# Strip attention with another timetable: three of the sixteen chunk products of each strip are given other patches

## The chip, the cores and the metric

The kernel runs on one core of one Trainium2 chip. The metric is the device time of one launch in microseconds, the median of some runs; the profile is of one further execution. The engines are PE (TensorE; its weight loads are listed as PEld), DVE (VectorE), ACT (ScalarE), POOL (GpSimd) and SP (SyncE), which here only issues transfers.

## What is computed

```python
# x: (2, 96, 256, 256); windows of 16x16 with step 14: 19 rows x 19 columns for each of 2 images
tok = crop.transpose(...).reshape(b * n, 256, 96)
y = _layernorm(tok, norm1_w, norm1_b)
q, k, v = y @ wq, y @ wk, y @ wv            # 4 heads, 16 values per head for q and k, 24 for v
attn = softmax(q k^T / 4)                   # 256 x 256 for each head and window
tok = (attn @ v) @ wproj + tok              # and back into the image, overlaps halved
...
y = _gelu(y @ fc1_w + fc1_b)                # per pixel, then a 5x5 depthwise conv, gelu, fc2
...
t = t + ffn(_ln_t(t))                       # two small quantized linear layers
```

## The kernel before, in words

The program has three stages, one behind the other: `norm_stage` (the first norm), `attention_stage` and `map_stage` (all that is done per pixel and the convolution). The change touches only numbers that `attention_stage` reads.

`attention_stage` works in 38 strips (2 images x 19 rows of windows, 16 pixels high, 256 wide), each with 19 windows, called patches here and numbered 0 to 18. For each patch j there is a fixed cycle:

- PE turns the row maxima of patch j (L661), makes the first two heads' scores of patch j+1 (L654), and, in some patches, one product for a whole chunk (below).
- DVE forms the query row `QF` of patch j (L815), which needs L661. PE then makes the transposed scores of patch j (L669, needs `QF`) and the last two heads' scores of j+1 (L654).
- DVE takes the row maxima of j+1 in two halves (L820), each as soon as PE's scores are there; the second half is the last thing before PE can begin patch j+1.
- ACT does the exponential (L768), copies `V` (L750) and the output `OS` (L758); PE weighs the values (L677) and makes the next values (L645).

Beside that, a strip is 8 chunks of 32 columns. For each chunk there is one product for q and k (`queries_keys`, L633, called a QK product here), and, later, one projection (`project`, L641). Both write one bank of PSUM, `B_CK`, so that they alternate with whoever empties it:

- A QK product is copied by ACT to `QS` (L746), then cast by DVE to `QB` (L806, "Q" below), while SP moves its half to `KS` with four transfers (L396), from which DVE makes `KB` (L810, "K" below).
- A projection is added by DVE to the image rows in `XHS` (L839, "R" below). The projections of chunks 4 to 7 of a strip are made in the next strip's patches.

Two tables set the patch in which PE makes each product, `QK_STEP` for the QK products and `OUT_STEP` for the projections. DVE does R in the patch of the projection, Q one patch after the QK product, K two patches after it (chunk 1: one). In a patch DVE does R, Q, the softmax shares (L829 and L833, "S" below, after patches 2, 6, 11 and 16) and K in this order, behind the second row maximum and ahead of the next `QF`. A K of chunk 6 is first needed by the scores of patch 13, which PE makes in patch 12.

SP works its own queue in a fixed order. In the middle of a strip it is: shares of the first 5 patches (L404, L411, L415), fetch of the left half of the next strip (L440), keys of chunk 6 (L396), store of the right half of the strip before (L428, after all its R), then the sums of patches 5 to 9 (L404 `RSC<-OS`, after ACT's copy of patch 9's output). POOL adds up the outputs of a group of patches (L552 to L568) when the shares are back, and behind group 0 it makes four chunks of the next strip's normalised input `Y` (L505).

Of the kernel before, what the change touches and what calls it, by code (L numbers as in the profile page):

```python
# [250 lines left out]
            blocks(dve, body)  # L251


QK_STEP = {2: 0, 3: 2, 4: 4, 5: 6, 6: 8, 7: 10, 0: 15, 1: 17}
OUT_STEP = {4: 3, 5: 5, 6: 7, 7: 9, 0: 12, 1: 14, 2: 16, 3: 18}
GROUPS = ((0, 5), (5, 10), (10, 15), (15, NPOS))
GROUP_STEP = (6, 11, 16, 2)
ROUND = 6
# [5 lines left out]
def attention_stage(nc, xhat, rnorm, n1w, n1b, wq, wk, wv, wproj, ident, share, qrows, sums, x2map, nstrip=NSTRIP):  # L264

    ctx = ExitStack()
    with ctx:
# [349 lines left out]
        def _(pe):  # L617
# [31 lines left out]
            def scores(j, *hs):  # L649

                for half in range(2):
                    for h in hs:
                        hr = slice(32 * h, 32 * h + 32)
                        m = T.matmul(P[:, B_S[h], half * PT:(half + 1) * PT],  # L654
                                     QB[hr, win(j, half * 128, half * 128 + 128)], KB[hr, win(j)], start=True, stop=True)
                m.then_inc(pe_s, 1)
# [25 lines left out]
            def body(s, n, k, prev, follow):  # L682
                kept, outs = 2, -4
                for j in range(NPOS):
# [7 lines left out]
                    if more:  # L692
                        pe.wait_ge(dve_kb, n(s, NCK, NCK * ((j + 1) // NPOS) + first_new(nj) + 1))
                        scores(nj, 0, 1)
                    for c, at in QK_STEP.items():
                        if at == j and (c > 1 or follow):
                            queries_keys(s + (c < 2), n, c, n(s, NCK, outs) if prev or outs > 0 else None)
                            kept += 1
                    for c, at in OUT_STEP.items():
                        if at == j and (c < 4 or prev):  # L700
# [37 lines left out]
        def _(act):  # L738
# [21 lines left out]
            def body(s, n, k, prev, follow):  # L760
                for j in range(NPOS):
                    par = (s * NPOS + j) % 2
                    for c, at in QK_STEP.items():
                        if at == j and (c > 1 or follow):
# [19 lines left out]
        def _(dve):  # L784
# [32 lines left out]
            def row_max(s, n, j):  # L817
                for i in range(2):
                    dve.wait_ge(pe_s, n(s, 2 * NPOS, 2 * j + i + 1))
                    V_.tensor_reduce(NM[:, :, :].rearrange("p a (u d) -> p u a d", d=32)[:, 2 * i:2 * i + 2, :, DQ],  # L820
                                     P[:, B_S[0]:B_S[0] + 2, :].rearrange("p u (a m) -> p u a m", a=2), axis=AX.X, op=ALU.max)\
                      .then_inc(dve_max, 1)

            def shares(s, n, q, first):

                j0, j1 = GROUPS[q]
                r = RS[:, q % 2, 0:8 * (j1 - j0)]
                dve.wait_ge(sums_in, n(s, 256, 64 * q + 64))
                V_.reciprocal(r, r).then_inc(dve_rs, 1)  # L829
                if q == 0 and not first:  # L830
                    dve.wait_ge(sh_loaded, n(s, 16, 0))
                dve.wait_ge(dve_rs, n(s, 4, q + 1))
                V_.tensor_tensor(r, r, SH[:, 8 * j0:8 * j1], ALU.mult).then_inc(dve_rsh, 1)  # L833

            def residual(s, n, c):

                dve.wait_ge(pe_out, n(s, NCK, c + 1))
                x = XH[:, s % 2, :, c * CKC:(c + 1) * CKC]
                V_.tensor_tensor(x, P[0:C + 1, B_CK, :].rearrange("c (w r) -> c r w", r=PATCH), x, ALU.add).then_inc(dve_out, 1)  # L839

            def body(s, n, k, prev, follow):
                for j in range(NPOS):
                    query_row(s, n, j)
                    if follow or j < LAST:
                        row_max(s, n, j + 1)
                    for c, at in OUT_STEP.items():
                        if at == j and (c < 4 or prev):
                            residual(s - (c > 3), n, c)
                    for c, at in QK_STEP.items():
                        if at == j - 1 and (c > 1 or follow):  # L850
                            queries16(s + (c < 2), n, c)
                    for q, at in enumerate(GROUP_STEP):
                        if at == j and (q < 3 or prev):
                            shares(s - (q > 2), n, q, not prev)
                    for c, at in QK_STEP.items():
                        if at == j - (2 if c != 1 else 1) and (c > 1 or follow):
# [820 lines left out]
```

## Time and profile before

| | |
|---|---|
| median of 3 runs | 8434.09 us (8430.1 to 8454.12) |
| the profiled execution | 8441.3 us |
| its span | 8439.5 us |
| granted TensorE clock, mean | 0.975 |
| busy: PE, DVE, ACT, POOL | 7670.8, 4919.9, 4683.4, 2161.9 us |
| attention stage | from about 519 to 3890 us of the span |

PE is listed as busy for nine tenths of the span, but in the attention stage its instructions are short and many of them end only after a wait that is not shown as idle between the pieces of one product. The stage is a ring of PE and DVE, so it is read patch by patch: the time between two starts of L815 is the length of a patch. A group of the profile such as `L810 DVE TENSOR_SCALAR` is all K operations together. In a timeline, the brackets at the end of a row give how long the engine was idle before it and whose work ended that.

### The profile page before, as it was taken

What the parts mean: (1) busy time and instruction counts of PE and PEld (TensorE: products, weight loads), DVE (VectorE), ACT (ScalarE), POOL (GpSimd) and SP (SyncE); (2) the same over time, 40 slices, a digit from 0 to 9 for tenths busy, and PEclk for the clock granted to TensorE, in tenths of its full rate; (3) what the DMA queues carried; (4) which work ended last, traced back from release to release, by engine and by line L of the source; (5) the groups of instructions that cost most, each with busy time, mean ns of one, the idle gap of its engine ahead of it and who ended that gap; (6) DMA issues with size and microseconds to landing.
All of it is one profiled execution on the core that took longest, in us unless ns stands there. A gap on an engine that the chain in (4) does not pass through costs nothing.

```text
span 8439.5 us, 205332 instructions
## 1 busy us (share of the span) xinstructions
PE 7670.8 (91%) x77004; PEld 4600.6 (55%) x77004; DVE 4919.9 (58%) x8231; ACT 4683.4 (55%) x7546; POOL 2161.9 (26%) x1712
## 2 busy tenths in 40 slices
PE   8969999999999999996989898989989898989898
PEld 3335555555455555554666666666666666666665
DVE  7867777777777777775344444444444444444444
ACT  6636555566565565653555454545454545455554
POOL 0023434434343343342112121212121212111111
PEclk9979999999999999997999999999999999999999
DMA  7734444444344443432111111111111111111110
GB/s 213 231 99 103 95 100 98 98 98 99 92 106 96 99 102 92 105 93 72 33 43 37 43 37 43 37 43 37 43 37 40 39 36 44 33 43 35 43 37 26
DMA packets 403125, 611.55 MB, mean 72 GB/s; under 512 B 95641, under 2 KB 338171, under 8 KB 377695
## 3 DMA queue, kind: packets, MB, share of 16 engines
q1 hardware_dynamic: 402639, 604.98, 28.9%
q8 instruction: 316, 5.18, 0.3%
q14 instruction: 170, 1.39, 0.1%
HBM read 395.33 MB, written 166.64 MB: 67 GB/s over the span
## 4 chain that ended last, share of the span: by engine, by line
PE 30%; DVE 10%; ACT 8%; issue 5%; DVEq 0%; SPq 0%; DMA 0%; ACTq 0%; POOLq 0%; POOL 0%
PE P L1299 6%; PE P L1165 6%; PE P L1312 5%; ACT H L1372 4%; PE P L1220 4%; DVE H L1538 3%; PE P L1173 3%; DVE H L1531 2%; PE P L1328 2%; DVE Z L1553 2%; PE P L1139 2%; ACT Z L1397 1%; ACT L1397 1%; ACT L1360 1%; PE P L1199 1%
## 5 line engine op out<-in xcount | busy, mean ns | idle before, releaser
L820 DVE TENSOR_REDUCE NM<-P 128x4 f32<-128x1024 f32 x1444 | 1764.8, 1222 | 596.3 <-PE P L654 591.7
L768 ACT ACTIVATE PROB<-P 128x1024 f32<-128x1024 f32 x1444 | 1400.2, 1021 | 1025.0 <-PE P L669 1025.0
L1220 PE MATMUL P<-FC,XN 97*126 97x192 f32 x5408 | 1099.0, 342 | 15.7 <-ACT Y L1382 14.8
L1220 PEld LDWEIGHTS P<-FC,XN 97*126 97x126 f32 x5408 | 941.3, 196 | 168.2 <-issue 77.8
L669 PE MATMUL P<-QF,KS 32*128 32x256 f32 x11552 | 834.5, 403 | 111.0 <-DVE QF L815 110.4
L1366 ACT ACTIVATE SQ<-Z 96x512 f32<-96x512 f32 x260 | 163.8, 630 | 1286.3 <-DVE Z L1518 1286.3
L669 PEld LDWEIGHTS P<-QF,KS 32*128 32x128 f32 x11552 | 525.4, 185 | 635.7 <-DVE QF L815 572.7
L505 POOL TENSOR_TENSOR Y<-XHS,RNS 96x512 f32<-96x512 f32 x304 | 600.6, 2003 | 811.8 <-DMA RNS<-rnorm 513.9
L677 PE MATMUL P<-PROB,V 128*32 128x256 f32 x11552 | 776.9, 386 | 1.4 <-ACT PROB L768 1.4
L1382 ACT ACTIVATE Y<-P 126x384 f32<-126x384 f32 x1352 | 704.1, 569 | 109.3 <-PE P L1220 104.2
L1099 POOL TENSOR_TENSOR T<-T,Y 96x512 f16 (+1 forms) x260 | 299.5, 1152 | 1720.0 <-DVE Y L1542 1720.0
L1103 POOL COPY Z<-T 1x2560 f32 (+1 forms) x52 | 236.9, 4555 | 1892.6 <-PE P L1165 1892.6
L1312 PE MATMUL P<-Y,WC 127*64 127x52 f32 x19968 | 625.2, 223 | 28.3 <-ACT Z L1397 28.3
L1312 PEld LDWEIGHTS P<-Y,WC 127*64 127x64 f32 x19968 | 598.9, 138 | 63.1 <-ACT Z L1397 34.9
L1553 DVE TENSOR_TENSOR Z<-P,Z 96x400 f32<-96x400 f32 (+1 forms) x728 | 342.6, 533 | 432.5 <-PE P L1328 432.5
L654 PE MATMUL P<-KB,QB 32*128 32x256 bf16 x5776 | 563.9, 272 | 20.1 <-DVE KB L810 16.9
L1299 PE MATMUL P<-XN,FC 97*96 97x440 f32 x1248 | 540.2, 554 | 0.7 <-ACT Y L1382 0.7
L645 PEld LDWEIGHTS P<-WQKV,Y 97*128 97x128 f32 x2888 | 377.5, 190 | 298.2 <-issue 298.2
L1165 PE MATMUL P<-Z,FC 97*96 97x430 f32 (+1 forms) x1248 | 499.4, 529 | 41.8 <-DVE Z L1553 41.8
L645 PE MATMUL P<-WQKV,Y 97*128 97x128 f32 x2888 | 515.4, 301 | 0.0
L1372 ACT ACTIVATE H<-P 128x1536 f16<-128x1536 f32 x260 | 377.4, 1451 | 238.7 <-DVE H L1538 182.8
L552 POOL TENSOR_TENSOR EDGE<-OS,RBC 128x160 f32<-128x160 f32 (+2 forms) x152 | 74.9, 493 | 1677.1 <-DMA RBC<-sums 1661.0
(152 smaller groups left out, 11706.8 us busy)
## 6 DMA issues: line engine op xcount, KB each, us to landing
RBC<-sums SPq DMA_DIRECT2D x456, 160.0 KB, 3.1
X<-x2map SPq DMA_DIRECT2D x52, 1344.0 KB, 8.3
XHS<-xhat SPq DMA_DIRECT2D x76, 768.0 KB, 6.2
RNS<-rnorm SPq DMA_DIRECT2D x38, 1536.0 KB, 9.4
x2map<-XHS SPq DMA_DIRECT2D x76, 768.0 KB
T<-in_x SPq DMA_DIRECT2D x52, 960.0 KB
out<-T SPq DMA_DIRECT2D x52, 960.0 KB, 4.9
X<-in_x SPq DMA_DIRECT2D x32, 1536.0 KB, 8.9
```

Of the source, the lines that this page charges most:

```text
L505: G.tensor_tensor(Y[0:C, x, :], XH[0:C, s % 2, :, x].rearrange("c r w -> c w r"), RN[:, :, x].rearrange("c r w -> c w r"), ALU.mult).then_ ...
L645: v = T.matmul(P[:, B_OV, PT + half * 128:PT + half * 128 + 128], yf[:, win(j, half * 128, half * 128 + 128)], WQKV[:, 128:256], start=Tru ...
L669: m = T.matmul(P[:, B_ST[h], half * PT:(half + 1) * PT], KS[hr, win(j, half * 128, half * 128 + 128)], QF[hr, :], start=True, stop=True)
L677: m = T.matmul(P[32 * h:32 * h + 32, B_OV, 0:PT], V[:, par, half, 32 * h:32 * h + 32], PROB[:, par, h, half * PT:(half + 1) * PT], start=( ...
L768: A.activation(PROB[:, par, u:u + 2, :], P[:, B_ST[u]:B_ST[u] + 2, :], ACT.Exp, scale=DQ ** -0.5).then_inc(act_exp, 1)
L820: V_.tensor_reduce(NM[:, :, :].rearrange("p a (u d) -> p u a d", d=32)[:, 2 * i:2 * i + 2, :, DQ], P[:, B_S[0]:B_S[0] + 2, :].rearrange("p ...
L1165: m = M.matmul(P[0:C, j % 2, 0:px.stop - px.start], FC2[0:C + 1 - half, half, :], Z[0:C + 1 - half, half, px], start=(half == 0), stop=(ha ...
L1220: m = M.matmul(P[0:KW, 5 + (r + 2) % 3, i * MLP:(i + 1) * MLP], xnf[:, RI * WX * w:RI * WX * w + KW], FC1[:, :], start=True, stop=True)
L1299: M.matmul(P[0:C, 6 + k % 2, 0:(x1 - x0) * RO], FC1[:, half * C:(half + 1) * C], XN[:, 2 + x0:2 + x1, 2:2 + RO], start=True, stop=True).th ...
L1312: m = M.matmul(P[64 * half:64 * half + 64, 2 * (q % 2) + i // GP, (i % GP) * NWIN:(i % GP + 1) * NWIN], WC[:, (half * C + c) * MW:(half * ...
L1372: A.activation(H16[:, :, :], P[:, 0:3, :], ACT.Copy).then_inc(act_h, 1)
L1382: A.activation(Y1[0:KW, :, 2 * r:2 * r + 2], P[0:KW, 5 + (r + 2) % 3, 0:2 * MLP].rearrange("p (w c) -> p c w", w=2), ACT.Gelu).then_inc(ac ...
```

## The change

Chunk 6's QK product goes from patch 8 to patch 7, its projection from patch 7 to patch 8, and the projection of chunk 0 from patch 12 to patch 13, in which PE had none.

```diff
-QK_STEP = {2: 0, 3: 2, 4: 4, 5: 6, 6: 8, 7: 10, 0: 15, 1: 17}
-OUT_STEP = {4: 3, 5: 5, 6: 7, 7: 9, 0: 12, 1: 14, 2: 16, 3: 18}
+QK_STEP = {2: 0, 3: 2, 4: 4, 5: 6, 6: 7, 7: 10, 0: 15, 1: 17}
+OUT_STEP = {4: 3, 5: 5, 6: 8, 7: 9, 0: 13, 1: 14, 2: 16, 3: 18}
```

Nothing is added or removed; the orders of SP and POOL stay as they were. What the tables move on the other engines is seen in the order of the instructions.

DVE, the first strip inside the loop, from the end of patch 9 to the end of patch 10, before (`XHS<-P1,XHS` is R, `QB<-QS` is Q, `KB<-KS,MSK` is K; `REGISTER_ALU` rows count up what is waited for):

```order
276 L837 REGISTER_ALU
277 L839 TENSOR_TENSOR XHS<-P1,XHS 97x16x32
278 L805 REGISTER_ALU
279 L806 CAST QB<-QS 128x512
280 L814 REGISTER_ALU
281 L815 SCALAR_TENSOR_TENSOR QF<-QS,MSK,P1 128x256
282 L819 REGISTER_ALU
283 L820 TENSOR_REDUCE NM<-P1 128x2x2
284 L819 REGISTER_ALU
285 L820 TENSOR_REDUCE NM<-P1 128x2x2
286 L810 TENSOR_SCALAR KB<-KS,MSK 128x512
```

And now, from the end of patch 8 (the R of chunk 6 is the row ahead of these) to the end of patch 9:

```order
269 L805 REGISTER_ALU
270 L806 CAST QB<-QS 128x512
271 L810 TENSOR_SCALAR KB<-KS,MSK 128x512
272 L814 REGISTER_ALU
273 L815 SCALAR_TENSOR_TENSOR QF<-QS,MSK,P1 128x256
274 L819 REGISTER_ALU
275 L820 TENSOR_REDUCE NM<-P1 128x2x2
276 L819 REGISTER_ALU
277 L820 TENSOR_REDUCE NM<-P1 128x2x2
278 L837 REGISTER_ALU
279 L839 TENSOR_TENSOR XHS<-P1,XHS 97x16x32
280 L810 TENSOR_SCALAR KB<-KS,MSK 128x512
```

Before, patch 7 ended with R and Q, patch 8 with K, patch 9 with R and Q, patch 10 with K. Now patch 7 ends with Q, patch 8 with R, Q and K, patch 9 with R and K, and patch 10 with nothing; K of chunk 6 is the last row here, a patch earlier than row 286 of before.

PE, the same strip, patches 7 to 8, before (`P1<-ACCO,WP` is the projection, L628, L632 and L637 are counts of waits ahead of a product):

```order
291 L641 MATMUL P1<-ACCO,WP 97x512
292 L705 REGISTER_ALU
293 L669 MATMUL P1<-QF,KS 128x256 x8
294 L710 REGISTER_ALU
295 L654 MATMUL P1<-KB,QB 128x256 x4
296 L677 MATMUL P1<-PROB,V 32x256 x8
297 L645 MATMUL P1<-WQKV,Y 128x128 x2
298 L688 REGISTER_ALU
299 L661 MATMUL P1<-IDN,NM 128x128 x2
300 L654 MATMUL P1<-KB,QB 128x256 x4
301 L628 REGISTER_ALU
```

And now (`P1<-Y,WQKV` is the QK product):

```order
291 L633 MATMUL P1<-Y,WQKV 128x512
292 L705 REGISTER_ALU
293 L669 MATMUL P1<-QF,KS 128x256 x8
294 L710 REGISTER_ALU
295 L654 MATMUL P1<-KB,QB 128x256 x4
296 L677 MATMUL P1<-PROB,V 32x256 x8
297 L645 MATMUL P1<-WQKV,Y 128x128 x2
298 L688 REGISTER_ALU
299 L661 MATMUL P1<-IDN,NM 128x128 x2
300 L654 MATMUL P1<-KB,QB 128x256 x4
301 L637 REGISTER_ALU
302 L641 MATMUL P1<-ACCO,WP 97x512
```

The two products of chunk 6 have changed places.

PE, patches 12 to 13, before:

```order
343 L654 MATMUL P1<-KB,QB 128x256 x4
344 L637 REGISTER_ALU
345 L641 MATMUL P1<-ACCO,WP 97x512
346 L705 REGISTER_ALU
347 L669 MATMUL P1<-QF,KS 128x256 x8
348 L710 REGISTER_ALU
349 L654 MATMUL P1<-KB,QB 128x256 x4
350 L677 MATMUL P1<-PROB,V 32x256 x8
351 L645 MATMUL P1<-WQKV,Y 128x128 x2
352 L688 REGISTER_ALU
353 L661 MATMUL P1<-IDN,NM 128x128 x2
354 L654 MATMUL P1<-KB,QB 128x256 x4
```

And now:

```order
343 L654 MATMUL P1<-KB,QB 128x256 x4
344 L705 REGISTER_ALU
345 L669 MATMUL P1<-QF,KS 128x256 x8
346 L710 REGISTER_ALU
347 L654 MATMUL P1<-KB,QB 128x256 x4
348 L677 MATMUL P1<-PROB,V 32x256 x8
349 L645 MATMUL P1<-WQKV,Y 128x128 x2
350 L688 REGISTER_ALU
351 L661 MATMUL P1<-IDN,NM 128x128 x2
352 L654 MATMUL P1<-KB,QB 128x256 x4
353 L637 REGISTER_ALU
354 L641 MATMUL P1<-ACCO,WP 97x512
```

The projection of chunk 0 stands one patch later, ahead of patch 13's L669. Its R goes with it, from the end of patch 12, where a K stands as well, to the end of patch 13, where DVE had nothing.

## Rows read from the trace of the kernel before

**Rows 1.** Windows: busy time of each engine in the attention stage

```profile
519.00:3890.00 3371.00, 3221.67 (x34418) 1698.20 (x34418) 2568.51 (x3376) 2007.78 (x3193) 1323.76 (x1330) 0.99 0.42 97
```

**Rows 2.** Waits of the attention stage: us in total, times, longest us

```profile
PEld P L669 <- DVE QF L815: 572.7, 668, 2.5
...
DVE RSC L829 <- DMA RSC<-OS: 63.5, 67, 2.0
```

**Rows 3.** Timeline of strip 10, DVE, `QF` of patches 13, 14 and 15

```profile
1477.83 0.47 DVE L815 SCALAR_TENSOR_TENSOR QF<-QS,MSK,P 128x256 f32<-128x256 f32 x1
...
1481.79 0.48 DVE L815 SCALAR_TENSOR_TENSOR QF<-QS,MSK,P 128x256 f32<-128x256 f32 x1 [0.63 <-PE P L661]
...
1486.30 0.48 DVE L815 SCALAR_TENSOR_TENSOR QF<-QS,MSK,P 128x256 f32<-128x256 f32 x1
```

**Rows 4.** Timeline of strip 10, PE: L669 of patch 13, projection of patch 14

```profile
1478.36 1.15 PE L669 MATMUL P<-QF,KS 32*128 32x256 f32 x16 [0.52 <-DVE QF L815]
...
1482.01 1.10 PE L641 MATMUL P<-ACCO,WP 128*97 128x512 f32 x2
```

**Rows 5.** Timeline of strip 10, DVE, from patch 7's `QF` to patch 11's

```profile
1450.11 0.48 DVE L815 SCALAR_TENSOR_TENSOR QF<-QS,MSK,P 128x256 f32<-128x256 f32 x1
...
1453.35 0.68 DVE L839 TENSOR_TENSOR XHS<-P,XHS 97x512 f32<-97x512 f32 x1
1453.94 0.42 DVE L806 CAST QB<-QS 128x512 bf16<-128x512 f32 x1
1454.28 0.48 DVE L815 SCALAR_TENSOR_TENSOR QF<-QS,MSK,P 128x256 f32<-128x256 f32 x1
...
1457.88 0.48 DVE L810 TENSOR_SCALAR KB<-KS,MSK 128x512 bf16<-128x512 f32 x1
1458.60 0.48 DVE L815 SCALAR_TENSOR_TENSOR QF<-QS,MSK,P 128x256 f32<-128x256 f32 x1 [0.24 <-PE P L661]
...
1463.32 0.47 DVE L815 SCALAR_TENSOR_TENSOR QF<-QS,MSK,P 128x256 f32<-128x256 f32 x1
...
1466.93 1.49 DVE L810 TENSOR_SCALAR KB<-KS,MSK 128x512 bf16<-128x512 f32 x1
1468.34 0.47 DVE L815 SCALAR_TENSOR_TENSOR QF<-QS,MSK,P 128x256 f32<-128x256 f32 x1
```

**Rows 6.** Timeline of strip 10, PE: the QK product of patch 8

```profile
1454.28 1.13 PE L633 MATMUL P<-Y,WQKV 97*128 97x512 f32 x2
```

**Rows 7.** Timeline of strip 10, DVE, `QF` of patch 18 and the next

```profile
1500.16 0.48 DVE L815 SCALAR_TENSOR_TENSOR QF<-QS,MSK,P 128x256 f32<-128x256 f32 x1 [0.24 <-PE P L661]
...
1505.27 0.48 DVE L815 SCALAR_TENSOR_TENSOR QF<-QS,MSK,P 128x256 f32<-128x256 f32 x1
```

**Rows 8.** Timeline of strip 10, POOL, from group 0 to the `Y` chunks

```profile
1457.95 0.72 POOL L552 TENSOR_TENSOR EDGE<-OS,RBC 128x128 f32<-128x128 f32 x1 [14.21 <-DMA RBC<-sums]
...
1460.32 3.18 POOL L565 TENSOR_TENSOR ACCO<-OS,RBC 128x980 f32<-128x980 f32 x2 [0.18 <-POOL ACCO L562]
...
1464.21 8.00 POOL L505 TENSOR_TENSOR Y<-XHS,RNS 96x512 f32<-96x512 f32 x4
```

**Rows 9.** Groups of the attention stage: all K operations

```profile
L810 DVE TENSOR_SCALAR KB<-KS,MSK 128x512 bf16<-128x512 f32 x304 | 188.9, 621 | 2.1 <-DMA KS<-QS 2.1
```

**Rows 10.** Timeline of strip 10, SP: keys of chunk 6; their time to landing

```profile
1456.14 3.06 SPq L396 DMA_DIRECT2D KS<-QS  x4
...
KS<-QS SPq DMA_DIRECT2D x4, 32.0 KB, 4.5
```

**Rows 11.** Timeline of strip 10, SP: gathering the sums of patches 5 to 9

```profile
1468.18 3.00 SPq L404 DMA_DIRECT2D RSC<-OS  x4
```

**Rows 12.** Timeline of strip 10, DVE, end of patch 11

```profile
1471.57 0.92 DVE L806 CAST QB<-QS 128x512 bf16<-128x512 f32 x1
1473.05 0.40 DVE L829 RECIPROCAL RSC<-RSC 128x40 f32<-128x40 f32 x1 [0.56 <-DMA RSC<-OS]
...
1473.60 0.47 DVE L815 SCALAR_TENSOR_TENSOR QF<-QS,MSK,P 128x256 f32<-128x256 f32 x1
```

## Prediction

> **What bounds the kernel now.** I read the windows by stage first. The attention stage, the only one that the change touches, takes 3371 of the 8439.5 us at a granted clock of 0.99, and there PE is at 3221.67 us, DVE at 2568.51, POOL at 1323.76 [rows 1]. So no engine is idle for long, and none is simply full. The waits of the stage come next: PE's weight loads of L669 wait for the query row `QF` 668 times, 572.7 us in all [rows 2], about once in each of the 722 patches. The ring is therefore PE, DVE, PE, DVE, and the measure is the time from one L815 to the next.
>
> The timeline gives that measure. Patch 13, with no product, R, Q, K or S, takes 1481.79 - 1477.83 = 3.96 us [rows 3]: the floor. Two shadows lie in the ring. DVE sits idle 0.63 us ahead of `QF` until PE's L661 is done [rows 3], so DVE can do something there for nothing. How much: patch 7 ends with R and Q, which from R's start to `QF`'s take 1454.28 - 1453.35 = 0.93, and the patch takes 1454.28 - 1450.11 = 4.17, 0.21 over the floor [rows 5]; so 0.72 of DVE's extra work is free. From start to start R is 0.59, Q 0.34 [rows 5], K (0.48 us long, less the same 0.08 of overlap) 0.40. Alone each is free; R and K together are 0.27 over, which patch 12 shows, 1477.83 - 1473.60 = 4.23 [rows 3, 12]; R, Q and K together are 1.33, 0.61 over.
>
> The second shadow is PE's. A projection stands between L654 and L669. In patch 14, behind a patch without DVE extras, it makes 1486.30 - 1481.79 = 4.51, so it costs 0.55 [rows 3]; L669 begins 0.53 after `QF` in the bare patch [rows 3, 4], and the projection's 1.10 us from 1482.01 [rows 4] push it back. Where the DVE work at the end of the patch before delays `QF`, that delay hides as much of the product. A QK product is as long, 1.13 [rows 6]; behind patch 7's 0.21 it costs 0.36 in patch 8 (1458.60 - 1454.28 = 4.32, K free) [rows 5], so 0.57 in the open.
>
> **The change, part by part.** Strip 10 in its own numbers, then the sum. I go from patch 7's `QF`.
>
> - Patch 7. Its product stands behind K and S of patch 6, and was hidden (4.17 is all R and Q). With the QK product there it is hidden again. At its end only Q is left, free. 4.17 becomes 3.96: -0.21.
> - Patch 8. The projection of chunk 6 now stands behind a lone Q, so nothing hides it: 0.55. At the end stand R, Q and K: 0.61. 3.96 + 0.55 + 0.61 = 5.12 where 4.32 was: +0.80. The same case stands in the trace, patch 18 (projection behind a lone K; R, Q and K at the end): 1505.27 - 1500.16 = 5.11 [rows 7].
> - Patch 9. Chunk 7's projection had cost 0.55 behind patch 8's lone K, and R and Q 0.21: 1463.32 - 1458.60 = 4.72 [rows 5]. Now it is behind 0.61 and hidden; R and K cost 0.27: 4.23, that is -0.49.
> - Patch 10 took 1468.34 - 1463.32 = 5.02 [rows 5]: 0.36 of QK product behind R and Q, and 0.7 of K, which here takes 1.49 us and not 0.48, while POOL makes the `Y` chunks (8.00 us from 1464.21) [rows 5, 8]. Now no K, and 0.57 - 0.27 = 0.30 of product: 4.26, -0.76.
>
> So far -0.66. But the gain at patch 10 comes at its very end, and it does not stay. Behind patch 11 stands S, which waits 0.56 us for `RSC<-OS` [rows 12], and SP begins that gather at 1468.18 [rows 11], after ACT's copy of patch 9's output, which hangs on patch 10's L669 and not on patch 10's K. L669 of patch 10 moves by -0.21 + 0.80 - 0.49 = +0.10 for `QF`, and -0.06 for the product (0.30 for 0.36): +0.04. So S and with it patch 12's `QF` come 0.04 later, not 0.66 earlier: the stall goes from K to S. S waits for this transfer 67 times in 152 [rows 2]. Where it does not, Q of patch 11 (0.92 for 0.42 us [rows 5, 12]) is held until POOL's last `Y` chunk is done, 1464.21 + 8.00 = 1472.2 [rows 8], and coming earlier gives it nothing either. Then:
>
> - Patch 12 loses its projection, which the long S had hidden, and its R: 4.23 becomes 3.96, -0.27.
> - Patch 13 gets it behind a lone K: +0.55, and a free R: 4.51. Patch 14 keeps 4.51, since its predecessor's lone R delays no `QF`.
>
> Per strip: 0.04 - 0.27 + 0.55 = +0.32, and 37 strips have all of it: 11.8 us.
>
> Two costs come from K and Q meeting other work. First the transfers: the four key transfers of chunk 6 are issued from 1456.14 to 1459.20 and take 4.5 us to land, so the last, issued at about 1458.6, lands at 1463.1 [rows 10]; K would now start at 1458.60 + 0.59 + 4.23 - 0.40 = 1463.02. With the product a patch earlier SP may begin them up to 0.3 earlier. Bounds: 0 and 0.3; in the whole stage K waited 2.1 us for its keys [rows 9]. I take 0.04, 1.5 us. Second POOL: Q of chunk 6 and K of chunk 5 now fall at about 1458.4 to 1459.3, on POOL's short pieces from 1457.95 on [rows 8]. Nothing bounds that from below but 0; from above by one piece, about 0.5 us a strip or 18 us. K as a whole takes 621 ns on average [rows 9] for 479 undisturbed (0.48), so I take 0.14, 5 us.
>
> Sum: 11.8 + 1.5 + 5 = 18 us on the profiled execution's 8441.3, which is 7 above the median. On the median: 8434 + 18 = 8452. ACT's copy of q and k comes with its product and stays ahead of the exponential; its order and that of SP and POOL add nothing.
>
> On K's 1.49 us the row shows that it starts in one `Y` chunk and ends after it. The Trainium skill, "SBUF — State Buffer", Who interferes with whom, states that DVE in a 2-port mode and GpSimd take the shared port pair for a whole instruction, and the other blocks. The trace agrees (1.49 against 0.48); by that rule a K that comes late by a little would lose up to a whole `Y` chunk, which is the second rival.
>
> **The rivals.**
>
> 1. S does not take the gain back. If the gather came earlier or S were seldom the last, all terms stay: -0.66 - 0.27 + 0.55 = -0.38 a strip, 14 us faster, 8420. For it: 85 of the 152 S did not wait. Against: S at patch 11 did in strip 10, and Q's 0.92 is tied to POOL's clock. To be measurably faster it would take twice as much.
> 2. Slower: chunk 6's K meets the first `Y` chunk. It would end at about 1463.5, and that chunk starts at 1464.21 [rows 8], 0.7 us later. If it starts first, K waits its 2.0 us (8.00 / 4), less the 0.30 of product that this hides: +1.6 on patch 10's L669, so on the gather and on S. In each strip that is 60 us, in half of them 30: 8482. It decides from some 5 strips in 37 on (18 + 5 x 1.6 = 26 us). For it: 0.3 us of late keys and 0.5 us of POOL's pieces together use up the 0.7. Against: POOL's `Y` chunks do not get earlier, since group 0 starts on a transfer that the change leaves alone.
> 3. The ring's terms cancel fully and only noise is left (both S and POOL's clock pull patches 7 to 11 to nought, and patch 13's product is partly hidden): 0 to 5 us, 8437.
>
> **How the numbers follow.** The forecast gets 0.5, the first rival 0.13, the second 0.2, the third 0.13, and 0.04 is left for a gain that I don't see. A measurement of this kernel can tell 0.3%, 25 us, from no change (its three times lie 24 us apart). Slower by more: the second rival and a little of the forecast's upper side, 0.23. Faster by more: 0.05. Within: 0.72. Range: down to 8425, between the first and third rival with its spread, up to 8485, the second at half the strips.
>
> **What would show it.** `QF` to `QF` in patch 7 to 10, 12 and 13: 3.96, 5.12 to 5.3, 4.23, 4.26, 3.96, 4.51. K of chunk 6 at 0.48 and no longer 1.49, at the end of patch 9. More waiting of S for `RSC<-OS`: 67 waits become about 80 and 63.5 us some 15 more. If K of chunk 6 shows 1 to 2 us, the second rival holds. The prediction is wrong if patch 8 is well under 5.1, or patch 11 does not grow by what patch 10 loses.

## The result and the profile after

The changed kernel takes 8485.62 us (median of 5 runs, 8477.42 to 8491.36) against 8434.23 (the kernel before, now also 5 runs): ratio 1.0054, 95% interval 1.0043 to 1.0065. It is slower, by about 45 us. The profiled execution takes 8477.4 us, 36 more than that of before; its attention stage, from the first `QF` to the last, takes 3386.2 us against 3351.7, and what comes before and behind it is as long as it was within 2 us. So nearly all of it is in the stage that was changed. The 36 us are less than the 45 because the profiled execution of before lies 7 us above its median and that of the changed kernel, the fastest of its five, 8 us below.

The window of the stage and the two waits, after. The columns, as in [rows 1, 2]: the window and its length; busy us and (number of instructions) of PE, PEld, DVE, ACT and POOL; granted clock, DMA share, GB/s.

```profile
519.00:3930.00 3411.00, 3250.51 (x34422) 1708.71 (x34420) 2565.82 (x3378) 2008.88 (x3193) 1325.38 (x1333) 0.98 0.41 96
```

```profile
PEld P L669 <- DVE QF L815: 581.2, 671, 3.1
...
DVE RSC L829 <- DMA RSC<-OS: 59.2, 59, 7.9
```

The busy time of the other engines is the same within 3 us, PE's is 29 us more though its products are the same, and PE's granted clock is 0.98 where it was 0.99. That is the first trace of what the prediction had not seen.

The time from one L815 to the next, as a mean over strips 1 to 36, shows where the time went. It is worked out from the 722 rows of L815 in each trace; the two ends of the list are the same in kind as [rows 3]. Patches that are not in the table differ by less than 0.15; the largest of them is patch 6, 0.12 shorter.

| patch | 7 | 8 | 9 | 10 | 11 | 12 | 13 | whole strip |
|---|---|---|---|---|---|---|---|---|
| before | 4.17 | 4.37 | 4.81 | 4.81 | 4.94 | 4.25 | 3.96 | 88.25 |
| changed | 4.00 | 5.27 | 4.66 | 4.09 | 5.23 | 4.60 | 4.51 | 89.22 |
| forecast (undisturbed) | 3.96 | 5.12 | 4.23 | 4.26 | taken back | 3.96 | 4.51 | |

The same in one strip, DVE in strip 12 of the changed kernel, from patch 8's `QF` to patch 13's R:

```profile
1640.70 0.48 DVE L815 SCALAR_TENSOR_TENSOR QF<-QS,MSK,P 128x256 f32<-128x256 f32 x1 [0.30 <-PE P L661]
...
1644.49 0.68 DVE L839 TENSOR_TENSOR XHS<-P,XHS 97x512 f32<-97x512 f32 x1
1645.09 0.42 DVE L806 CAST QB<-QS 128x512 bf16<-128x512 f32 x1
1645.42 0.48 DVE L810 TENSOR_SCALAR KB<-KS,MSK 128x512 bf16<-128x512 f32 x1
1645.82 0.47 DVE L815 SCALAR_TENSOR_TENSOR QF<-QS,MSK,P 128x256 f32<-128x256 f32 x1
...
1649.66 0.85 DVE L810 TENSOR_SCALAR KB<-KS,MSK 128x512 bf16<-128x512 f32 x1
1650.43 0.47 DVE L815 SCALAR_TENSOR_TENSOR QF<-QS,MSK,P 128x256 f32<-128x256 f32 x1
...
1654.38 0.48 DVE L815 SCALAR_TENSOR_TENSOR QF<-QS,MSK,P 128x256 f32<-128x256 f32 x1 [0.63 <-PE P L661]
...
1657.63 1.74 DVE L806 CAST QB<-QS 128x512 bf16<-128x512 f32 x1
1659.29 0.39 DVE L829 RECIPROCAL RSC<-RSC 128x40 f32<-128x40 f32 x1
1659.71 0.20 DVE L833 TENSOR_TENSOR RSC<-RSC,SH 128x40 f32<-128x40 f32 x1
1659.83 0.47 DVE L815 SCALAR_TENSOR_TENSOR QF<-QS,MSK,P 128x256 f32<-128x256 f32 x1
...
1665.21 0.48 DVE L815 SCALAR_TENSOR_TENSOR QF<-QS,MSK,P 128x256 f32<-128x256 f32 x1 [0.67 <-PE P L661]
```

Patch 8 is 1645.82 - 1640.70 = 5.12, as forecast. K of chunk 6 takes 0.85 us and not 1.49 [rows 5], and patch 10 takes 3.95: its QK product lies behind `QF`, which this K, still longer than 0.48, holds back, and at its end DVE has nothing. But Q of patch 11 takes 1.74 us where the row of before has 0.92 [rows 12]. POOL shows why, same strip:

```profile
1651.31 7.78 POOL L505 TENSOR_TENSOR Y<-XHS,RNS 96x512 f32<-96x512 f32 x4
```

The `Y` chunks end at 1651.31 + 7.78 = 1659.09, and Q, begun at 1657.63, ends at 1659.37. Of what K no longer loses to POOL, Q now loses a part. The groups of the whole stage say the same, K and Q after, and Q before (columns: busy us, mean ns, idle before; K before is in [rows 9]):

```profile
L810 DVE TENSOR_SCALAR KB<-KS,MSK 128x512 bf16<-128x512 f32 x304 | 164.3, 540 | 10.2 <-DMA KS<-QS 10.1
L806 DVE CAST QB<-QS 128x512 bf16<-128x512 f32 x304 | 162.6, 535 | 22.3 <-ACT QS L746 22.3
```

```profile
L806 DVE CAST QB<-QS 128x512 bf16<-128x512 f32 x304 | 148.2, 488 | 22.0 <-ACT QS L746 22.0
```

K as a whole loses 24.6 us, Q gains 14.4.

The last line of strip 12 above is the surprise: patch 12, with nothing but a free K, takes 5.38 us, not 3.96. The windows of patches 11 and 12 of this strip:

```profile
1654.38:1659.83 5.45, 4.00 (x50) 2.06 (x47) 4.92 (x6) 3.03 (x6) 4.71 (x3) 1.00 0.09 19
1659.83:1665.21 5.38, 4.85 (x44) 2.88 (x46) 3.23 (x6) 2.16 (x3) 0.00 (x0) 0.68 0.49 137
```

The clock is 0.68 over patch 12: 0.32 x 5.38 x 2 = 3.4 us of it at 1.2 GHz instead of 2.4. PE's own rows there, the last product of patch 11 and then patch 12:

```profile
1658.24 0.39 PE L654 MATMUL P<-KB,QB 32*128 32x256 bf16 x4
1660.36 2.09 PE L669 MATMUL P<-QF,KS 32*128 32x256 f32 x16 [1.73 <-DVE QF L815]
1662.24 0.63 PE L654 MATMUL P<-KB,QB 32*128 32x256 bf16 x4
1662.81 1.50 PE L677 MATMUL P<-PROB,V 128*32 128x256 f32 x16
1664.24 0.71 PE L645 MATMUL P<-WQKV,Y 97*128 97x128 f32 x4
```

PE had idled 1.73 us for `QF`, behind Q and S, and then L669 takes 2.09 us where it takes 1.15 in [rows 4]. In 16 of strips 1 to 36 patch 12 is like this, 5.41 us on average, and in the other 20 it is 3.96. In the kernel before it never is. Patch 11 was 5.45 us on average ahead of such a patch 12 and 5.06 ahead of the others.

The idle time of PE ahead of L669 goes with it, but does not settle it alone: it was 1.39 to 2.08 us ahead of the 16, and 1.01 to 1.97 us ahead of the other 20. Strip 3, where the clock fell, and strip 10, where it did not:

```profile
861.50 2.04 PE L669 MATMUL P<-QF,KS 32*128 32x256 f32 x16 [1.39 <-DVE QF L815]
```

```profile
1483.98 1.15 PE L669 MATMUL P<-QF,KS 32*128 32x256 f32 x16 [1.97 <-DVE QF L815]
```

### The profile page after: what moved, and what is told of

Its sections match the earlier page's. It is cut to its first block, busy times and chain, and to the rows that moved or that the text cites. A ratio compares the mean times of both kernels' runs of the same rounds, so it can differ in the third digit from the quotient of the medians.

```text
span 8475.6 us, 205332 instructions
## 1 busy us (share of the span) xinstructions
PE 7698.2 (91%) x77004; PEld 4610.7 (54%) x77004; DVE 4916.8 (58%) x8231; ACT 4683.9 (55%) x7546; POOL 2160.2 (25%) x1712
## 3 DMA queue, kind: packets, MB, share of 16 engines
q14 instruction: 170, 1.39, 0.1%
## 4 chain that ended last, share of the span: by engine, by line
PE 30%; DVE 10%; ACT 8%; issue 5%; DVEq 0%; DMA 0%; SPq 0%; ACTq 0%; POOLq 0%; POOL 0%
PE P L1299 6%; PE P L1165 6%; PE P L1312 5%; ACT H L1372 4%; PE P L1220 4%; DVE H L1538 3%; PE P L1173 3%; DVE H L1531 2%; PE P L1328 2%; DVE Z L1553 2%; PE P L1139 2%; ACT Z L1397 1%; ACT L1397 1%; ACT L1360 1%; PE P L1199 1%
## 5 line engine op out<-in xcount | busy, mean ns | idle before, releaser
L669 PE MATMUL P<-QF,KS 32*128 32x256 f32 x11552 | 844.4, 407 | 117.0 <-DVE QF L815 115.9
L669 PEld LDWEIGHTS P<-QF,KS 32*128 32x128 f32 x11552 | 529.8, 187 | 642.8 <-DVE QF L815 581.2
```

The costliest lines, as they stand in the source:

```text
L669: m = T.matmul(P[:, B_ST[h], half * PT:(half + 1) * PT], KS[hr, win(j, half * 128, half * 128 + 128)], QF[hr, :], start=True, stop=True)
```

## The experiments

Theory A: chunk 6's move is nearly neutral, as forecast; moving chunk 0's projection costs its 0.28 us a strip and, on top, takes from patch 12 the product without which PE's granted clock falls there. Rival B: the fall needs both parts of the change. Rival C: patch 12 is long for another reason and the clock only comes with it. All kernels ran in rounds with the kernel before on the same chip. "Falls" are patches 12 of strips 1 to 36 over 4.9 us in the profiled execution, all at the lower clock; "long idle" counts the strips of these 36 in which PE idled 1.23 us or more ahead of patch 12's L669 (1.23 is the shortest idle time ahead of any fall here); "attention" is from its first `QF` to its last. The mean granted clock is that of all timed executions, not of the profiled one alone.

| kernel | median us | ratio (95%) | attention us | falls | long idle | mean clock |
|---|---|---|---|---|---|---|
| before | | 1 | 3351.7 | 0 | 0 | 0.975 |
| changed | 8485.6 | 1.0054 (1.0043 to 1.0065) | 3386.2 | 16 | 26 | 0.970 |
| e11, changed again | 8487.6 | 1.0050 (1.0037 to 1.0064) | 3399.4 | 13 | 25 | 0.970 |
| e1, chunk 0's part only | 8468.1 | 1.0037 (1.0025 to 1.0049) | 3373.8 | 9 | 11 | 0.972 |
| e2, chunk 6's part only | 8444.8 | 1.0006 (0.9998 to 1.0015) | 3361.8 | 0 | 0 | 0.974 |
| e3, changed + product in patch 12 | 8462.7 | 1.0036 (1.0023 to 1.0049) | 3360.4 | 0 | 1 | 0.974 |
| e8, changed + product in patch 11 | 8467.7 | 1.0037 (1.0023 to 1.0051) | 3381.0 | 4 | 7 | 0.973 |
| e4, changed, chunk 0 in patch 11 | 8447.2 | 1.0015 (1.0006 to 1.0023) | 3370.4 | 5 | 14 | 0.974 |
| e6, changed, S of patch 11 in 12 | 8444.4 | 1.0007 (0.9998 to 1.0016) | 3353.8 | 0 | 1 | 0.974 |
| e5, before, chunk 0 in patch 11 | 8441.6 | 1.0006 (0.9997 to 1.0015) | 3345.1 | 3 | 7 | 0.973 |
| e9, e5 with S in 12 | 8436.6 | 0.9996 (0.9987 to 1.0005) | 3340.5 | 0 | 1 | 0.974 |
| e10, e2 with chunk 7's product in 11 | 8447.4 | 1.0006 (0.9997 to 1.0015) | 3354.1 | 0 | 0 | 0.973 |
| e7, before with chunk 7's product in 11 | 8432.1 | 0.9991 (0.9982 to 1.0000) | 3341.8 | 0 | 0 | 0.975 |

Taken together, the 13 profiled executions have 468 such strips: in the 375 with an idle time under 1.23 us the clock never fell at patch 12, and in the 93 others it fell 50 times. The kernels without falls at patch 12 have at most one strip with so long an idle time.

**e1 and e2: each part alone.**

e1 against before:

```diff
-OUT_STEP = {4: 3, 5: 5, 6: 7, 7: 9, 0: 12, 1: 14, 2: 16, 3: 18}
+OUT_STEP = {4: 3, 5: 5, 6: 7, 7: 9, 0: 13, 1: 14, 2: 16, 3: 18}
```

e2 against before:

```diff
-QK_STEP = {2: 0, 3: 2, 4: 4, 5: 6, 6: 8, 7: 10, 0: 15, 1: 17}
-OUT_STEP = {4: 3, 5: 5, 6: 7, 7: 9, 0: 12, 1: 14, 2: 16, 3: 18}
+QK_STEP = {2: 0, 3: 2, 4: 4, 5: 6, 6: 7, 7: 10, 0: 15, 1: 17}
+OUT_STEP = {4: 3, 5: 5, 6: 8, 7: 9, 0: 12, 1: 14, 2: 16, 3: 18}
```

> Only the projection of chunk 0 moves, from patch 12 to 13; chunk 6 stays as before. Ring terms alone: -0.27 in patch 12 and +0.55 in patch 13, +0.28 us in each of 38 strips, 11 us, ratio 1.0013. Theory A (the clock: with patches 11 and 12 without a product PE's granted clock falls to its lower level at the start of patch 12 in some strips, 1.4 us each, as in the changed kernel): half-speed stretches at patch 12 in 10 to 17 strips, 25 to 35 us in all, ratio 1.003 to 1.004. Rival B (the fall of the clock needs the longer stall of patch 11 that moving chunk 6 makes, its Q of 1.3 to 1.8 us): few or none at patch 12, ratio 1.001 to 1.0015.

> Only chunk 6's two products change places; the projection of chunk 0 stays in patch 12. Ring terms: patches 7 to 11 come to +0.04 us plus what POOL takes from the K of patch 8, up to 0.2, so 2 to 8 us, ratio 1.000 to 1.001. Theory A and rival B both want no clock fall at patch 12, since a product stands there; if half-speed stretches at patch 12 or 11 appear all the same, the stall of patch 11 alone is enough and the ratio is 1.003 or more.

Measured: 1.0037 with 9 falls, and 1.0006 with none. In e1 the fall is there with patch 11 as it was before on average (4.93 us for 4.94), so rival B is out; the windows of patches 11 and 12 in one of its strips:

```profile
1469.09:1474.80 5.71, 3.87 (x50) 2.05 (x46) 4.15 (x8) 2.90 (x6) 3.83 (x2) 1.00 0.09 18
1474.80:1480.33 5.53, 5.00 (x44) 2.79 (x46) 3.23 (x6) 2.37 (x4) 0.00 (x0) 0.69 0.49 131
```

Still the longer patch 11 counts: 9 falls here, 16 and 13 with chunk 6 moved too. In e1 patch 11 took 5.59 us ahead of a fall and 4.71 ahead of the rest. In e2 patch 11 is 5.30 on average, longer than in the changed kernel, with no fall: the projection stands in patch 12, and PE's idle time ahead of L669 is 1.09 us at most. Its patches 7 to 11 are 4.00, 5.25, 4.57, 4.12 and 5.30, together 0.15 over before: chunk 6's move is worth 5 us in the trace's strips 1 to 36, against 0.04 + 0.14 + 0.04 forecast, 8 us. The stage of this execution is 10 us longer than before; over 8 of them are in its last strip (90.3 us for 81.7), where the clock was at half in patch 9 and in patch 17.

**e3 and e8: a product too much.** The changed kernel with chunk 0's projection made once more, its first result unused, in patch 12 (e3; e8 has `j == 11` there):

```diff
+                    if j == 12:
+                        pe.wait_ge(pool_grp, n(s, 4, 1))
+                        pe.wait_ge(act_qs, n(s, NCK, kept))
+                        if prev or outs > 0:
+                            pe.wait_ge(dve_out, n(s, NCK, outs))
+                        T.matmul(P[0:C + 1, B_CK, :], WP[:, :], af[:, ck(0)], start=True, stop=True)
                     pe.wait_ge(dve_qf, n(s, NPOS, j + 1))
```

> The changed kernel with one projection product more in patch 12 of every strip (chunk 0's product made twice, the first result unused). Theory A: the half-speed stretches at patch 12 go, patch 12 stays near 3.96 to 4.1 in all strips, and the kernel gets 20 to 25 us faster than the changed one although PE does more: ratio to before 1.0025 to 1.0035. Rival C (patch 12 is long for another reason, a transfer or POOL, and the clock only comes with it): the same strips still take 5.4 us there, ratio 1.006 or more.

> The changed kernel with the extra, unused projection product in patch 11 instead of patch 12. Tells whether the bare patch 12 or the product-free stall of patch 11 ahead of it makes the clock fall. If work ahead of the stall is enough: few falls at patch 12 (under 4), ratio 1.001 to 1.003. If patch 12's own product is what counts: falls at patch 12 stay at 10 to 17, ratio 1.004 to 1.006.

With more work for PE in patch 12 the kernel is faster than the changed one: by its ratio 1.0036 for 1.0054 and 1.0050, 12 to 15 us, with intervals that overlap, so that the timed runs alone do not show it; by the attention stage of the profiled executions, 3360.4 for 3386.2, 25.8 us, twice what the two profiled executions of the changed kernel differ by (13.2). The ratio as a whole is not explained: e3's stage is only 9 us longer than before's, its profiled execution is its fastest, and its others take up to 25 us more at nearly the same clock (0.973 to 0.975). Strip 10, patches 11 and 12, windows and then PE (L710 is the extra product, L821 its `QF`):

```profile
1469.71:1475.19 5.48, 5.03 (x52) 2.30 (x48) 4.96 (x6) 3.03 (x6) 4.74 (x3) 1.00 0.09 17
1475.19:1479.15 3.96, 3.43 (x44) 2.05 (x46) 3.23 (x5) 2.16 (x3) 0.00 (x0) 1.00 0.35 98
```

```profile
1473.89 1.10 PE L710 MATMUL P<-ACCO,WP 128*97 128x512 f32 x2
1475.72 1.15 PE L669 MATMUL P<-QF,KS 32*128 32x256 f32 x16 [0.73 <-DVE QF L821]
```

Patch 11 is as long as in strip 12 of the changed kernel (5.48 and 5.45), but PE begins the product of patch 12 while DVE is still at Q and S, idles 0.73 us and not 1.73, the clock stays at 1.00, L669 takes 1.15 us and patch 12 takes 3.96, in all 36 strips (in the others PE idles 0 to 1.24 us). Rival C is out: nothing but PE's own work differs. The price of the falls in the changed kernel is then 16 x (5.41 - 3.96) = 23 us. e8, with the product ahead of the stall instead of in it, still has 4 falls and 1.0037; its patch 12 is 4.13 on average. It helps in part, and the run fits neither of its two expected cases; its last strip was over 6 us longer than before's (88.1 for 81.7), with the clock at half for 13.65 us from its patch 9 on.

**e4 and e5: chunk 0's projection in patch 11.**

e4 against changed (e5 does the same to before):

```diff
-OUT_STEP = {4: 3, 5: 5, 6: 8, 7: 9, 0: 13, 1: 14, 2: 16, 3: 18}
+OUT_STEP = {4: 3, 5: 5, 6: 8, 7: 9, 0: 11, 1: 14, 2: 16, 3: 18}
```

> The changed kernel with the projection of chunk 0 in patch 11, whose end waits for the sums anyway. Ring: the product and its R lie in that wait, in full or in part; patches 12 and 13 are both bare, 3.96 each, so 0.27 less than before in patch 12 and 0.55 less than the changed kernel in patch 13. Without clock falls: ratio 0.998 to 1.001. Theory A as first put (two patches in a row without a product): falls at patch 13, some 1.4 us each, ratio 1.001 to 1.004. If instead the fall needs a patch 11 that stalls and has no product, none, ratio under 1.001.

> The kernel before with only the projection of chunk 0 in patch 11 instead of 12. Ring: in patch 11 product and R lie in the time until the sums are there in those strips where S waits for them, and cost up to 0.3 us where Q of patch 11 is the last; patch 12 falls from 4.25 to 3.96. -0.25 to +0.1 us a strip, -10 to +4 us. Clock: patches 12 and 13 have no product, so some falls at patch 12, as in the run with the changed kernel and this same patch (6): +8 us. Ratio 0.999 to 1.001. If the clock falls come only from the changed kernel's longer stall, none, ratio 0.998.

Patches 12 and 13 are bare in both. The falls are at patch 12 (5 and 3), not at patch 13 where "two patches in a row without a product" had put them: that form of the theory was wrong. What counts is the stall at the end of patch 11 and what PE has right behind it: with a product ahead of the stall instead, the clock still falls behind idle times of 1.23 to 1.97 us. For the rest the ring's rule held: patch 11 grows by 0.22 and 0.08 with the product and R in it (5.23 to 5.45; 4.94 to 5.02), patch 13 stays at 3.97.

**e6 and e9: without S behind patch 11.** e6 against changed; e9 is e5 with the same line changed.

```diff
-GROUP_STEP = (6, 11, 16, 2)
+GROUP_STEP = (6, 12, 16, 2)
```

> The changed kernel with the shares of group 1 (S) behind patch 12 instead of 11. Theory (S takes back what patch 10 gains, since its sums land at a time of their own): without S patch 11 ends when Q is done, 0.5 us a strip earlier; patch 12 then ends with S, whose sums are long there, 0.55 us of which about 0.3 is over the shadow. Net -0.2 to -0.3 us a strip, 8 to 11 us faster than the changed kernel. The rest of patch 11's stall is POOL's last Y chunk, which stays, so patch 11 keeps 4.6 to 4.8 us. Clock: S's delay now precedes patch 13's product; falls at patch 12 should stay, 10 or more. Ratio to before 1.003 to 1.005. Rival (S is not what holds patch 11): patch 11 stays at 5.2.

> The kernel before with the projection of chunk 0 in patch 11 and the shares of group 1 behind patch 12: a candidate. Patch 11: product hidden behind the long K of patch 10, R and Q at its end, Q held by POOL, 4.6 to 4.9 (4.94 before). Patch 12: no product, S and K, 4.2 (4.25). Patch 13 bare, 3.96. Patch 16 may grow by 0.3 as in the changed kernel with this S. No clock falls at patch 12, as patch 11 has no wait for sums. -0.1 to -0.4 us a strip, ratio 0.998 to 1.000. If falls at patch 12 or 13 appear, two bare patches alone are enough for them.

e6 is the changed kernel but for this one number, and 40 us faster than it (by their ratios to before; the intervals are far apart). I had expected the falls to stay; there is none. Patch 11 is 4.46 and no longer 5.23, so S did hold it. In strip 12, from patch 11's `QF` on:

```profile
1646.44 0.48 DVE L815 SCALAR_TENSOR_TENSOR QF<-QS,MSK,P 128x256 f32<-128x256 f32 x1 [0.63 <-PE P L661]
...
1649.69 1.76 DVE L806 CAST QB<-QS 128x512 bf16<-128x512 f32 x1
1651.37 0.47 DVE L815 SCALAR_TENSOR_TENSOR QF<-QS,MSK,P 128x256 f32<-128x256 f32 x1
...
1654.61 0.39 DVE L829 RECIPROCAL RSC<-RSC 128x40 f32<-128x40 f32 x1
1655.03 0.20 DVE L833 TENSOR_TENSOR RSC<-RSC,SH 128x40 f32<-128x40 f32 x1
1655.15 0.48 DVE L810 TENSOR_SCALAR KB<-KS,MSK 128x512 bf16<-128x512 f32 x1
1655.55 0.47 DVE L815 SCALAR_TENSOR_TENSOR QF<-QS,MSK,P 128x256 f32<-128x256 f32 x1
```

Q is held by POOL as long as before (1.76), but without S behind it `QF` comes 1651.37 - 1646.44 = 4.93 after the last, and the bare patch 12 keeps its clock: PE idles 1.24 us ahead of its L669 at most, where the changed kernel has up to 2.08. Patch 13 gains too (4.27 for 4.51), since S and K ahead of it hide a part of its projection. A part comes back later: patch 16, where the next group's S and its product stand, is 5.83 us against 5.44 in the changed kernel, and 5.93 in e9 (5.53 before). e9 is level with before; its patch 11 is 4.37, less than the 4.6 to 4.9 expected.

**e7 and e10: chunk 7's QK product in patch 11**, the two best uses of the ring's rule that I could find.

e7 against before (e10 does the same to e2):

```diff
-QK_STEP = {2: 0, 3: 2, 4: 4, 5: 6, 6: 8, 7: 10, 0: 15, 1: 17}
+QK_STEP = {2: 0, 3: 2, 4: 4, 5: 6, 6: 8, 7: 11, 0: 15, 1: 17}
```

> The kernel before with the QK product of chunk 7 in patch 11 instead of 10; Q of chunk 7 goes to patch 12, behind POOL's Y chunks, its K to patch 13. By the ring's rule: patch 10 loses 0.36 (product behind R and Q), patch 11's product is hidden behind K of chunk 6 (1.3 us long on average), patch 11 has no Q to be held by POOL and ends with S at once when the sums are there, which are gathered 0.36 us earlier; patch 12 has R and Q, 0.21 over, where it had R and K, 0.27; patch 13's K is free. -0.5 to -0.8 us a strip, 19 to 30 us faster, ratio 0.9965 to 0.998. Clock: patches 11 and 12 have products, so no falls at 12. Rival: the keys of chunk 7 come late for patch 14's scores and patch 13 or 14 grows by 0.3 or more, ratio 1.000.

> Chunk 6's two products changed as in the changed kernel, the projection of chunk 0 left in patch 12, and chunk 7's QK product in patch 11: a candidate. Patch 10 is bare, 3.96 (4.12 in the run with chunk 6 only); the gather starts up to 0.15 earlier; patch 11 has no Q for POOL to hold and ends when the sums are there, 4.8 to 5.0 (5.30); patch 12 has product, R and Q, 4.2 to 4.5 (4.23). -0.2 to -0.5 us a strip against chunk 6 only, ratio 0.998 to 1.000. Clock: products in 11 and 12, so no falls there.

e7 has the lowest ratio of the study, 0.9991, which is 7 us and not the 19 to 30 expected; its interval (0.9982 to 1.0000) touches no change. Patch 10 stays at 4.79, not 0.36 less: K of chunk 6 comes earlier and waits the longer for POOL, 1.62 us on average for 1.33 and 1.84 in strip 10:

```profile
1462.01 1.84 DVE L810 TENSOR_SCALAR KB<-KS,MSK 128x512 bf16<-128x512 f32 x1
...
1467.10 0.40 DVE L829 RECIPROCAL RSC<-RSC 128x40 f32<-128x40 f32 x1
1467.55 0.20 DVE L833 TENSOR_TENSOR RSC<-RSC,SH 128x40 f32<-128x40 f32 x1
1467.72 0.48 DVE L815 SCALAR_TENSOR_TENSOR QF<-QS,MSK,P 128x256 f32<-128x256 f32 x1
...
1472.44 0.47 DVE L815 SCALAR_TENSOR_TENSOR QF<-QS,MSK,P 128x256 f32<-128x256 f32 x1
```

Patch 11 does get shorter, 4.94 to 4.37. But then S hides patch 12's projection no more, and patch 12 is 1472.44 - 1467.72 = 4.72 = 3.96 + 0.55 + 0.21, where I had forgotten the 0.55. e10 has the same miss: patch 11 is 5.08 for e2's 5.30, patch 12 is 4.37 for 4.23, and it stays level with e2. No falls at patch 12, as expected, but three others that were not: the clock was at half in patch 10, now without a product and behind the late K of patch 9, in strips 5, 12 and 15, with PE idle 1.51 to 1.97 us ahead of L669. That is the same case in another patch. No candidate beats the kernel before by more than e7.

**e11: the changed kernel again.**

> The changed kernel once more beside the others, for how often the clock falls at patch 12 in another execution on another chip. Theory: 10 to 20 half-speed stretches at patch 12 again, none or one at patch 11 and 13, ratio 1.004 to 1.006. Rival (the 17 of the first profile were chance): under 5.

13 falls at patch 12, ratio 1.0050; one of the 13 lasts on through patch 13 (7.43 us), and two more are in patch 10. The falls belong to the kernel and not to one execution, which the mean clock of all ten timed executions of it, 0.968 to 0.971 for 0.972 to 0.976 of before, says too. (Its expected text speaks of 17: those are half-speed stretches at patch 12 in all 38 strips, one of them in the last strip, which is not in the table.)

## Why the prediction was right or wrong

The forecast of 8452 was 34 us too low; the measured 8485.6 lies at the very upper bound of its range, 8485 (by the ratio, 8434 x 1.0054 = 8480), and "slower by over 0.3%", which had a chance of 0.23, is what happened. The likeliest case was wrong, mainly by one thing that was missing: the clock. That the bound still held is luck, since it was set by the second rival, half of all strips hit by POOL, which is not what happened.

- The ring. The floor of 3.96, the two shadows and their prices held in undisturbed strips: patch 7 at 3.96, patch 8 at 5.12 (4.00 and 5.27 on average), patch 13 at 4.51. Patches 9 and 10 did not: 4.66 and 4.09 on average for 4.23 and 4.26, since K of chunk 6 is late and long, and then hides patch 10's product. Patches 7 to 11 together are about +0.16 a strip, where 0.04 and the two small costs, 0.22 in all, were forecast. This is the step on which the neutral result rested; the total is right, but in part by luck, as the next points show.
- The step "the stall goes from K to S". Right that the gain of patch 10 (-0.72) does not stay. But patches 7 to 10 together gained only about 0.13 and not 0.66, and patch 11 took 0.29. Wrong in what takes it: I expected more waits of S for its sums, 80 for 67, and there are 59 (at patch 11 itself 11 for 14). Q of patch 11 took it, 0.87 us long on average before and 1.32 after. e6 shows that S on top of it still matters.
- POOL. Named as the second rival in the form "K of chunk 6 meets the first `Y` chunk". That happened in few strips: this K is 0.70 us on average (1.33 before), over 1.1 us in 5 of 36, which is 0.22 over its undisturbed 0.48. The rival gave the right sign and nearly the right time for the wrong reason. The term for K of chunk 5, 0.14, measured 0.02 in its own length (0.58 to 0.60); patch 8 is 0.15 over its undisturbed 5.12, this K being on the path now.
- Keys. K waits 10.1 us for transfers (2.1 before) where 1.5 more was forecast: 8 us more, all of it in ten strips' patch 9. Mis-sized: it is 0.2 of the 0.43 that patch 9 is over 4.23, and the 0.22 of POOL is the other half.
- Patch 12, "4.23 becomes 3.96, -0.27". This is the step that failed. It is 3.96 in 20 strips and 5.41 in 16, 4.60 on average: +0.35 instead of -0.27: 22 us over 36 strips. The profile before held the hint: the clock of the stage was not 1.00 but 0.99 [rows 1], and the kernel before has seven half-speed stretches there, five at the change of strips (patches 18 and 0) and two that begin in patch 11, which has no product, with PE idle 1.65 and 1.25 us ahead of L669. I summed patches at one clock and asked of the vacated patch only what it saves.
- The sum. 34.5 us in the stage of the profiled execution: 23 of falls at patch 12, and 11 for all the rest against 18 forecast. The profiled executions differ by some 10 us less than the timed ratio says. Executions of one kernel do differ by that much: in e11 the stage is 13 us longer than in the first profile, with 109 us at half clock in all for 96.

Shown by experiment: that chunk 0's part brings the falls (e1, e2), that PE's own work in patch 12 removes them (e3), and that the stall with S in patch 11 is needed for them in the changed kernel (e6). Both cures leave PE less idle time ahead of L669. Not shown: why one strip falls behind 1.39 us and another does not behind 1.97 us, and what the rest of e3's ratio is.

## What to carry to other kernels

A ring of two engines can be forecast from its own patches to a tenth of a microsecond: find the bare patch, the work that each engine may do in the other's shadow, and add what sticks out. That holds for undisturbed patches; late transfers and another engine's work moved single patches here by up to 0.4 us on average. But an empty slot on PE is no free slot: where it follows a stall, the product in it may be what keeps PE's idle time short and its clock up, and moving it away can cost more than the product did. So look at how long PE idles in the emptied slot, and not only at the slot's own price. And a gain ahead of something that runs on another clock (here POOL's 8 us of `Y` chunks, and the sums) can be taken back there, so look for the next such meeting point before adding it up.

## What the runs showed of the hardware that I had not expected

PE's granted clock fell from 2.4 to 1.2 GHz for 3.4 us after idle times as short as 1.39 us in the changed kernel and 1.23 us in e4, in a stage in which PE is listed as busy for over 95% of the time; L669 then took 2.04 to 2.09 us for 1.15 in the rows shown. It does not fall each time: at patch 12 it fell in 50 of the 93 strips, over all profiled executions, with 1.23 us or more, and in none of the 375 with less. With an extra, useless product begun 1.8 us earlier (idle time 0.73 us in the strip shown, at most 1.24) it did not fall there in any of 36 strips.

A DVE cast that began while POOL worked on a `Y` chunk ended only after that chunk: Q, 0.42 us undisturbed, took 1.74 us and ended 0.28 us after POOL's last `Y` chunk. The Trainium skill, "SBUF — State Buffer", Who interferes with whom, states that a DVE instruction in a 2-port mode and a GpSimd instruction take the shared port pair for a whole instruction, and that casts can be in such a mode if their operands allow it. The trace agrees (1.74 for 0.42).
